# A mixture of experts, attention and a second mixture of experts: VectorE's small operands in a PSUM bank, TensorE's narrow products spread over the units, and routing work in parts

## The reference, cut to what matters

```
x = x + 0.5 * ffn(layernorm(x))       # 8 experts, each row goes to the one with the greatest logit
x = x + attention(layernorm(x))       # blocks of 128 queries in batches of 4 tiles
x = x + 0.5 * ffn(layernorm(x))       # the same weights again

ffn(n):       e = argmax(n @ router.T); square(relu(n @ fc[e])) @ proj[e].T
attention(n): 16 heads of 8 channels, q @ k.T / sqrt(8), causal, head h sees the last max(4, 128 >> h) keys
              v = k; softmax; out * softmax(n @ Wgate + bgate) per head; @ Wproj + bproj
```

## Time and profile before

| | us |
|---|---|
| three runs | 444.8, 444.68, 442.11; median 444.68 |
| the profiled execution, its own time | 440.26 |
| its span, first to last instruction | 438.5 |
| PE, DVE, ACT, POOL busy | 357.5, 281.5, 263.5, 256.1 |
| mean granted TensorE clock | 0.952 of full speed |

### The profile page before, as it was taken

One profiled execution on the slowest core, in us unless ns is written; L12 is line 12 of the kernel. 1 busy time (PEld: TensorE's weight loads), 2 busy tenths in 40 slices (PEclk: granted clock), 3 DMA queues, 4 the chain that ended last, 5 costly groups with the idle time before them and its releaser, 6 DMA issues.

```text
span 438.5 us, 9118 instructions
## 1 busy us (share of the span) xinstructions
PE 357.5 (82%) x2634; PEld 333.2 (76%) x2643; DVE 281.5 (64%) x617; ACT 263.5 (60%) x684; POOL 256.1 (58%) x289
## 2 busy tenths in 40 slices
PE   5951049999998798779999999999475699999990
PEld 5941049999998477568879797989474699999990
DVE  4696014545566486999777979899996555545540
ACT  3370077667676586445787878686363367677650
POOL 5227747000174778487483847574977977765451
PEclk9999999999999999996999999999696599999996
DMA  9993113222242287417081822224022545722210
GB/s 244 405 270 91 54 54 102 77 66 61 78 120 73 67 184 153 100 33 161 19 169 29 172 61 40 58 41 98 12 100 96 140 125 160 198 82 63 58 29 1
DMA packets 82492, 45.40 MB, mean 104 GB/s; under 512 B 47117, under 2 KB 77455, under 8 KB 82209
## 3 DMA queue, kind: packets, MB, share of 16 engines
q1 hardware_dynamic: 77312, 34.38, 31.3%
q0 software_dynamic: 4864, 10.51, 7.6%
q10 hardware_dynamic: 288, 0.19, 0.2%
HBM read 24.48 MB, written 21.01 MB: 104 GB/s over the span
## 4 chain that ended last, share of the span: by engine, by line
PE 53%; POOL 20%; issue 9%; DVE 6%; ACT 5%; DMA 4%; SPq 1%; POOLq 0%; ACTq 0%; DVEq 0%
PE bank L1355 14%; PE bank L1346 14%; POOL rows_d L527 7%; PE bank L1433 5%; POOL late_rows_d L527 4%; POOL late L546 4%; PE bank L1465 3%; PE bank L1317 3%; PE bank L1443 2%; PE bank L1337 2%; PE bank L1306 2%; ACT sq L643 2%; ACT rows L626 2%; POOL rstd L574 2%; DMA rows<-in_x 1%
## 5 line engine op out<-in xcount | busy, mean ns | idle before, releaser
L1013 DVE TENSOR_SCALAR hT<-bank 128x512 f32<-128x512 f32 x80 | 55.3, 691 | 69.2 <-PE bank L1346 69.0
L1346 PE MATMUL bank<-xT,fcb 128*128 128x128 f32 x640 | 88.3, 283 | 5.6 <-ACT xT L659 5.6
L1355 PE MATMUL bank<-wo,hT 128*128 x640 | 87.9, 281 | 2.3 <-ACT hT L675 2.3
L1346 PEld LDWEIGHTS bank<-xT,fcb 128*128 128x128 f32 x640 | 81.2, 199 | 6.4 <-ACT xT L659 6.4
L1355 PEld LDWEIGHTS bank<-wo,hT 128*128 128x128 f32 x640 | 78.5, 193 | 3.1 <-issue 3.1
L669 ACT ACTIVATE fcb<-fc 128x512 f32 x80 | 50.2, 629 | 45.9 <-PE bank L1346 45.5
L546 POOL DMA_INDIRECT late<-y_d,slot x32 | 31.1, 973 | 51.1 <-DMA y_d<-ys 41.8
L537 POOL DMA_INDIRECT out_rows<-late x40 | 39.3, 983 | 24.9 <-DVE late L1022 17.9
L675 ACT ACTIVATE hT<-hT 128x512 f32<-128x512 f32 x80 | 50.1, 627 | 5.6 <-DVE hT L1013 5.2
L1433 PE MATMUL bank<-kT,qT 128*128 128x128 f32 (+4 forms) x256 | 48.5, 318 | 2.3 <-ACT late L754 2.0
L754 ACT ACTIVATE late<-bank,nmax 128x128 f32<-128x128 f32 (+2 forms) x128 | 46.5, 408 | 5.7 <-DVE nmax L1075 4.3
(11 more groups left out here) (158 smaller groups left out, 712.2 us busy)
## 6 DMA issues: line engine op xcount, KB each, us to landing
ks<-k_d SPq DMA_DIRECT2D x32, 192.0 KB, 3.3
late_rows_d<-hT SPq DMA_DIRECT2D x5, 1028.0 KB, 7.7
rows_d<-late SPq DMA_DIRECT2D x2, 1280.0 KB
xs<-rows_d SPq DMA_DIRECT2D x20, 128.0 KB
y_d<-ys SPq DMA_DIRECT2D x40, 64.0 KB
xs<-late_rows_d SPq DMA_DIRECT2D x20, 128.0 KB
fc<-in_w_fc SPq DMA_DIRECT2D x1, 2048.0 KB, 15.7
k_d<-qkg SPq DMA_DIRECT2D x8, 192.0 KB, 2.2
```

Source lines behind the costliest of these rows:

```text
L1013: nc.vector.tensor_scalar(hT[:, v, :, :].rearrange("p k c -> p (k c)"), bank[v][:, :], 0.0, None, ALU.max).then_inc(r_s, 1)
L1346: mm = pe.matmul(bank[v][:, k * 128:(k + 1) * 128], fcb[:, v, k * 128:(k + 1) * 128], xT[:, v, :], start=True, stop=True)
L1355: mm = pe.matmul(bank[OUT_BANK[f] + v][:, 0:128], hT[:, v, k, :], wo[:, ds(e, 1), k, :], start=(k == 0), stop=(k == KT - 1))
```

## The change

- **Operands in PSUM.** lmax, gmax, o4, den, rc and the part of fac for the light heads move from SBUF tensors into bank 2. fac becomes two products, one for the dense heads (`fac_d`, SBUF) and one for the light heads (`fac_l`, bank).
- **Narrow products.** `outputs(i, 0)` moves from unit 3 to unit 2, and `outputs(i, 1)` to the end of unit 3. The routing of a batch is one turn of four tiles in unit 0 (into bank 7), one ScalarE copy, and one set of logits in unit 4 (in batch 6 in unit 3), into bank 4, which also holds the outputs. `outputs(6, 2)` waits until the logits have been read.
- **First routing.** The inverse roots of the second segment are computed by VectorE with Newton steps (`spread`, existing code: two instructions and three steps of three) instead of GpSimd. The first scatter is in three parts of 6 tiles, each behind ScalarE's scaling of its rows. ScalarE's mask casts stand ahead of its second scaling.
- **Late choice and places.** `choose` becomes `find_best` (unit 4 of batch 6) and `choose_first` (unit 5). `place_tokens` becomes `place_first` (unit 0 of batch 7) and `place_rest` (unit 1), `place_blocks` goes from unit 1 to 4. TensorE's wait for these slots moves from a route turn in unit 1 of batch 7 to the turn of gated rows in unit 4.

```diff
+        small = {}
+        for n, a, w in (("lmax", 0, 48), ("gmax", 48, 4), ("o4", 64, 32), ("den", 96, 48), ("rc", 144, 64), ("fac_l", 208, 48)):
+            small[n] = bank[2][:, a:a + w]
...
-            for h in range(2):
-                roots(h + 1, SEG[0][h])
-                if h == 0:
-                    pool.wait_ge(zero_s, 48)
-                scatter(0, h, SEG[0][h], h + 1)
+            roots(1, SEG[0][0])
+            pool.wait_ge(zero_s, 48)
+            for k in range(3):
+                scatter(0, 0, slice(6 * k, 6 * k + 6), k + 1)
+            scatter(0, 1, SEG[0][1], 4)
             gather(0, 0, 14)
...
+            def route_copy_batch(q, b):
+
+                act.wait_ge(rt_px_s, GROUPS + q + 1)
+                act.wait_ge(logit_s, GROUPS + q)
+                act.activation(rT[:, :, :].rearrange("p u c -> p (u c)"), bank[b][:, :], ACT.Copy).then_inc(rt_T_s, 1)
...
+                if i >= 2 and n == 0:
+                    route_copy_batch(i - 2, 7)
...
-                if i >= 2 and n in (1, 2):
-                    route_copy(1, 2 * (i - 2) + n - 1, (2, 2))
...
-            normalise_rows(1, SEG[0][1].start, N_TILES)
-
             act.wait_ge(late_const_s, 16)
...
+            normalise_rows((rstd_s, 1), SEG[0][1].start, N_TILES)
...
-                step(nc.vector.tensor_tensor(fac[:, :, :], ge[:, u, :, :], rc[:, :, :], ALU.mult))
+                nc.vector.tensor_tensor(fac_d[:, :, :], ge[:, u, :, 0:DENSE], rc[:, :, 0:DENSE], ALU.mult)
+                step(nc.vector.tensor_tensor(fac_l, ge[:, u, :, DENSE:], rc[:, :, DENSE:], ALU.mult))
...
-                (6, 4): lambda: choose(1, 0, 2),
-                (6, 6): lambda: (count_blocks(1, 0, 2), bases(1, 0)),
-                (7, 0): lambda: place_tokens(1, 0, 2),
-                (7, 1): lambda: place_blocks(1, 0),
+                (6, 4): lambda: find_best(1, 0, 4),
+                (6, 5): lambda: choose_first(1, 0),
+                (6, 6): lambda: (count_blocks(1, 0, 6), bases(1, 0)),
+                (7, 0): lambda: place_first(1, 0, 6),
+                (7, 1): lambda: place_rest(1, 0),
+                (7, 4): lambda: place_blocks(1, 0),
...
-            scaled_variance(3, SEG[0][1])
             choose(0, 1, 3)
...
             place_blocks(0, 1)
+            spread(3, SEG[0][1])
...
+            def route_turn_batch(q, b):
+
+                pe.wait_ge(att_s, q + 1)
+                for t in range(4):
+                    mm = pe.transpose(bank[b][:, t * 128:(t + 1) * 128], x[:, 4 * q + t, :], ident)
+                mm.then_inc(rt_px_s, 1)
...
                 if i >= 3:
-                    pe.wait_ge(att_s, i - 2)
+
+                    pe.wait_ge(rt_T_s, GROUPS + i - 2)
                 pe.matmul(bank[7][:, :], wq4[:, :], xnT[:, i % 2, :], start=True, stop=True).then_inc(q_s, 1)
...
+                if i == B - 2:
+
+                    pe.wait_ge(slot_s, 3)
...
-                if n == 3:
-                    outputs(i, 0)
-                    outputs(i, 1)
                 if n == 5:
+                    if i == 6:
+
+                        pe.wait_ge(read_s, 3)
                     outputs(i, 2)
...
-                    g = 2 * (i - 2)
-                    if n in (2, 3):
-                        route_logits(1, g + n - 2, 2)
-                    if n in (1, 2):
-                        route_turn(1, g + n - 1, (2, 2))
+                if n in (2, 3):
+                    outputs(i, n - 2)
+                if i >= 2 and n == 0:
+                    route_turn_batch(i - 2, 7)
+                if i >= 2 and n == (3 if i == 6 else 4):
+                    route_logits_batch(i - 2)
```

146 lines of the change are left out of this document (77 added, 69 removed).

## The result

| | before | after |
|---|---|---|
| median (lowest to highest, runs) | 444.65 (442.11 to 450.86, 20) | 439.5 (436.8 to 448.14, 20) |
| ratio after to before, 95% interval | | 0.988 (0.986 to 0.991) |
| the profiled execution, its own time | 440.26 | 438.94 |
| its span | 438.5 | 437.1 |
| TensorE's mean granted clock in it | 0.952 | 0.932 |

What follows compares the result with a forecast made beforehand. It took four stretches in a row to bound the kernel: GpSimd's scatters first, TensorE in the expert stages, VectorE then TensorE in the attention. 8.0 + 1.0 + 0.4 - 1.4 = 8.0 us gave 432.3, plus 4.4 is 436.7; range 431 to 441.

Steps and rivals of the forecast that it cites:

- the likeliest case: Whole kernel: the prediction's own forecast, 436.7 us (432 to 440), chance 0.63.
- The first scatter's start, ScalarE's 14 rows, no stop for the roots: First routing: scatter starts at 26.6, 2.4 earlier; 14 rows take 4.2, to 48.1; later scatters follow without a stop.
- The first product, 7.3 us earlier: First expert stage: TensorE's first product comes at 53.8 instead of 61.09.
- So that idle goes too: 8.0 together: First expert stage, pair 5: the idle before its turn disappears, adding 0.65 to the 7.3 us.
- Part 1: First routing and scatter: second part's roots move from GpSimd to VectorE; the main gain, 8.0 us.
- PSUM operands, 1.1 us a batch, not dearer than SBUF: VectorE in the attention: products lose their stretch, saving 1.1 us a batch; writing a bank costs the short SBUF time.
- Narrow products, 0.1 a batch, a wait for the gate of 0.4 to 0.7: TensorE, batches 3 to 6: a gate wait of 0.4 to 0.7 replaces 0.6 idle, gaining 0.1 a batch.
- Batches 1 and 2, 1.0: Attention, batches 1 and 2: 1.0 us of VectorE's 3.0 gained; range 4 gained to 1 lost, depending on the clock.
- Batch 6, 0.1 gained: Attention, batch 6: its share of the 0.4 us put down for batches 3 to 6, at 0.1 a batch.
- Part 4, 1.4 late: Late choice and places: the scatter the second expert stage waits for comes 1.4 us late (0 to 3).
- The signs: Trace marks of a right forecast: first scatter near 26.6, first product near 54, dg 0.2, fcb 0.56, batches 20.2 long.
- The offset of 4.4 to the median: Whole kernel: the median lies 4.4 us above the profiled execution, so 432.3 becomes 436.7.

Runs made afterwards that it cites:

- combined_2: Changed kernel with late's edits, batch 2's first output set in unit 3, batch 6's logits read one unit earlier, first block placing behind the centring: 431.7 us, 0.967 of before.
- first_only: Kernel before with only the first-routing part of the change: 440.0 us, 0.989 of before.
- sbuf: Changed kernel with VectorE's six small operands back in SBUF, the bank left empty: 450.9 us, 1.015 of before.
- out3: Changed kernel with the first output set of each batch back in unit 3, beside the second: 441.9 us, 0.997 of before.
- rest0: Changed kernel with the last four steps of the late places back in unit 0 of batch 7, behind the first ones: 439.6 us, 0.988 of before.
- no_first: Changed kernel with the first-routing part undone, all other parts kept: 446.0 us, 1.004 of before.
- late_best3: late with the first output set in unit 3 from batch 6 on, and batch 6's logits read one unit earlier on VectorE: 440.0 us, 0.989 of before.
- late: Changed kernel with VectorE's late choice whole in unit 4 of batch 6, places whole in unit 0 and blocks in unit 1 of batch 7: 441.1 us, 0.991 of before.

## Why the prediction was right where it was right, and wrong where it was wrong

The time (436.7, range 431 to 441) came out at 439.5, and faster, as the likeliest case had it. But 5.2 us is two thirds of the 8.0, and of the profiled execution's 8.0 only 1.4 came. That the number came so near is in part luck, as the last point of this list shows. Step by step:

- **The first scatter's start, ScalarE's 14 rows, no stop for the roots:** right. 26.61 (26.6 forecast), 43.68 with 4.19 behind it (43.9 and 4.2), one GpSimd root less.
- **The first product, 7.3 us earlier:** 6.3. The failed step is "The first 18 end at 49.2": they ended at 50.29, since it takes the old scatters' pace to a new place. There the second and third run beside VectorE's centring, which cost 1.0. combined_2 gives 0.4 of it back by moving that centring. Before, scatters began at 28.99, after the first such product, and the second at 30.47, 0.07 before the end of the other: it had its usual 0.96.
- **"So that idle goes too: 8.0 together":** the idle before pair 5 went, and the first stage is only 0.1 shorter from its first product (81.52 against 81.60), so 0.65 was not a gain. Part 1: 6.4 at the end of the first stage, and 5.0 at the end of the kernel by first_only, 80 to 60% of the 8.0.
- **PSUM operands, 1.1 us a batch, not dearer than SBUF:** right. dg 0.21, fcb and scm 0.55. The maxima of 384 columns take 551 ns into a bank and 542 into SBUF (sbuf). The 48-column product with one operand in a bank takes 207 ns where the earlier trace rows have 0.22 for two in SBUF. The Trainium skill ("VectorE: DVE Perf Modes", the section on the TRN2 errata) gives 120 cycles for a PSUM source against 58. The trace doesn't agree, and it decides.
- **Narrow products, 0.1 a batch, a wait for the gate of 0.4 to 0.7:** 0.33 a batch in batches 3 to 5 (20.00 against 20.32 or more), with a wait of 0.24. Right in kind; sbuf and out3 show that the two parts only work together: with only one of them batches take 21.8 to 23.9 and 20.86, with neither (before) 20.32, with both 20.00. A sum with a price for each part hid this.
- **Batches 1 and 2, 1.0:** 0.1 lost in the trace. The range's lower end was the case: "TensorE would now wait for that gate", 4.19 us, with the low clock for 5.7 us behind it. rest0 has the same instructions in these batches, waits 2.4 and is 3.1 shorter. no_first has them too and waits as long as after, but its clock falls later (0.70 over the 5.7 us behind the wait, where after has 0.50), and it takes 74.45. So one trace could not tell the sign of this step: the wait and the clock behind it differ between executions. The first output set of batch 2 in no_first, 0.36 where after has 0.56:

```profile
206.57 0.36 PE L1503 MATMUL bank<-qkg,PT 128*128 128x9 f32 x2 [4.18 <-DVE fcb L1171]
```

- **Batch 6, 0.1 gained:** 1.09 lost. The wait for the read logits is in the change and was given no price. It should have had one: everything behind it in TensorE's queue waits, and TensorE paces this batch. late_best3 and combined_2, where the logits are read earlier, have it back.
- **Part 4, 1.4 late:** its own sum gives 1.6 (317.5 less 315.9), and the first late scatter came 3.6 later after the projection of batch 5 than before. The hand-over took 4.9 longer, the largest miss: 2.6 of it idle time, 2.2 the same products at a lower clock (0.71 against 0.80), for which the sum has no term. The idle time has three steps. "The scatter is what the second expert stage waits for": so it was, with the second routing 0.5 behind it, and that chain was late by nearly as much: with the scatter out of the way, in rest0, it alone holds the first product. The small steps of the places were taken at their old price: three products of eight columns took 0.92 instead of 0.17 and a fourth of 160 columns 1.19 instead of 0.33, 3.1 us in all, beside GpSimd's products. "What it gains lies beside 25 us of scatter: nothing": but the first output set moved ahead of unit 3's scores, and the blocks ahead of the shares of batch 7 put 2.0 us on the last gate. One scatter also took 2.72, beside VectorE's row of products from 321.11.
- **The signs:** dg and fcb, no root between scatters, first product near 54 and the clock at full speed from 215 to 295: all as written. Batches 3 to 5 were 20.0 long, batch 6 was not (21.4). The late scatter follows the cast of the slots by 0.87 (0.2 to 0.3 was written).
- **The offset of 4.4 to the median:** it belongs to one execution of before with an unusually high clock, and does not carry over. The median of after is 0.6 above its profile. A sum that had foreseen the 1.4 between the two traces, with this offset added, would have given 443.3, 3.8 above what was measured. The forecast gained too much in its terms and added too much in its offset, and the two misses went opposite ways: that is luck.

What stays open: in which stretches the ordinary executions of before lose their 4.4 us; what the disturbed chip waited for; how much of the hand-over's loss an edit can give back at the same clock (late against after says 3.8, against sbuf 1.9); and why TensorE's clock came back 10 us after the wait for the gate of batch 6 in combined_2 and in late (315.85, 320.97), but in late_best3 not before the second expert stage, behind a shorter wait.

## What to carry to other kernels

When two queues hand work to each other, price every wait that the edit adds, and what stands behind it in the queue, before pricing what it saves; the wait of 1.06 for a bank and the 2.0 of blocks ahead of the last gate cost more than all the batches gained. An edit that moves a consumer earlier and one that makes its producer faster are one edit, and are tested together. Where several small gains each seem to do nothing, put them together before dropping them: edits that could not be told from nothing by their times gave a ratio of 0.967 together, where the changed kernel has 0.988 (on the disturbed chip they gave nothing that can be told). And before a profiled execution stands for a kernel, look at its mean clock beside that of other executions.

## What the runs showed of the hardware that was not expected

- A scatter of GpSimd that starts beside a VectorE product of two SBUF operands (1.07 to 1.09 us) ends 0.84 us after that product's end, in three positions of three (29.23 after 28.39, 31.35 after 30.51, 29.64 after 28.80), whatever its own start. The one at 28.08 was held up by 0.2, the one at 29.54 by 0.85.
- Beside the row of five such products in batch 7 one scatter took 2.72 in after, 2.95 in rest0 and 2.68 in out3. In before and late the same row cost its scatters only 0.1 to 0.3 each:

```profile
324.92 1.08 POOL L527 DMA_INDIRECT late_rows_d<-rows,slot  x1 [0.30 <-issue]
321.55 1.29 POOL L530 DMA_INDIRECT late_rows_d<-rows,slot  x1 [0.30 <-issue]
```

  The first row is of before, the second of late. What decides between the two stays open.
- The stretch works the other way too, and hits small ones hardest: 128x8 products of VectorE took 0.92 instead of 0.17 beside GpSimd's products of 1.0 us.
- With the same instructions, executions differ by how long the lower clock lasts: batches 0 to 2 took 73.76 (rest0) to 78.49 (late), and behind a wait of 4.2 us the clock over the next 6 us was 0.50 in after and 0.53 in late, but 0.70 in no_first, whose batches 0 to 2 took 74.45. Six runs of combined_2 lie within 0.7%, where 18 of the changed kernel, on another chip, spread over 1.4%.
- A second stage that begins at the lower clock gives back part of what was won: from 342.11 on, late had 0.75 over 17.9 us, and its second stage took 82.39 where after's has 80.18. It isn't the early start: combined_2 begins at 336.69 with 0.91 over its first 13.3 us and takes 80.60.
